# Conv plus GRU on one core: the start-up re-ordered (Toeplitz tile in quarters, biases by a product, weights in whole rows over two queues)

## The reference, cut to what matters

```python
x = x + conv(x, cond[:, None, :]) + conv_b          # causal, per channel
def cell(h, x):
    gi = x @ W_ih + b_ih                            # 512 -> 1536
    gh = h @ W_hh + b_hh
    r, z = sigmoid(i_r + h_r), sigmoid(i_z + h_z)
    n = tanh(i_n + r * h_n)
    return (1 - z) * n + z * h
x = x + scan(cell, cond, x)
```

## Time and profile before

| What | Value |
|---|---|
| median of 3 runs | 1174.54 us |
| the profiled execution: its time, its span | 1172.44 us, 1170.6 us |
| TensorE (matmul) busy | 1116.4 us, 95% of the span |
| VectorE / ScalarE / GpSimd busy | 797.3 / 535.8 / 441.1 us |
| moved by DMA | 101.65 MB |
| first matmul of the early product | 30.04 us after the span's start |

### The profile page before, as it was taken

One profiled execution on the slowest core, in us unless ns is written; L12 is line 12 of the kernel. 1 busy time (PEld: TensorE's weight loads), 2 busy tenths in 40 slices (PEclk: granted clock), 3 DMA queues, 4 the chain that ended last, 5 costly groups with the idle time before them and its releaser, 6 DMA issues.

```text
span 1170.6 us, 15057 instructions
## 1 busy us (share of the span) xinstructions
PE 1116.4 (95%) x5254; PEld 933.0 (80%) x5254; DVE 797.3 (68%) x1231; ACT 535.8 (46%) x1012; POOL 441.1 (38%) x734
## 2 busy tenths in 40 slices
PE   1999999999999599999999999999999999999996
PEld 1977888888888487888888888888888888888885
DVE  2746676676774646677777777777777777777774
ACT  3536776777774153243443333343344333344332
POOL 0352112122012724344455554444455554444332
PEclk9999999999999889999999999999999999999999
DMA  9999899888845401011111111111111111111101
GB/s 249 280 233 190 183 195 191 187 191 194 189 122 122 102 21 35 18 37 36 37 36 36 37 34 30 30 35 36 37 37 36 37 34 30 30 34 37 28 19 27
DMA packets 233228, 101.65 MB, mean 87 GB/s; under 512 B 212944, under 2 KB 217552, under 8 KB 231104
## 3 DMA queue, kind: packets, MB, share of 16 engines
q1 hardware_dynamic: 212544, 66.11, 25.8%
q0 software_dynamic: 16256, 33.32, 10.4%
q10 hardware_dynamic: 4352, 1.25, 0.4%
HBM read 66.49 MB, written 34.14 MB: 86 GB/s over the span
## 4 chain that ended last, share of the span: by engine, by line
PE 91%; DMA 3%; DVE 3%; ACT 1%; issue 1%; ACTq 1%; SPq 0%; POOL 0%; DVEq 0%; POOLq 0%
PE bank L1095 55%; PE bank L1142 26%; PE bank L1117 5%; PE bank L1057 2%; PE bank L1084 2%; DMA w_again<-in_L_cond_W_ih_dram 1%; DVE comb L902 1%; DMA early<-early_result 1%; ACT toep_early L665 0%; DMA xres<-stage 0%; DMA tap_pad<-tap_rows 0%; SPq L480 0%; ACTq L641 0%; DVE comb_lo L929 0%; DMA xT<-early 0%
## 5 line engine op out<-in xcount | busy, mean ns | idle before, releaser
L1095 PE MATMUL bank<-w_hh_hi,hT_hi 128*128 128x512 f32 x768 | 299.7, 390 | 0.1
L1095 PE MATMUL bank<-w_hh_lo,hT_hi 128*128 128x512 f32 x768 | 299.4, 390 | 0.0
L1095 PE MATMUL bank<-w_hh_hi,hT_lo 128*128 128x512 f32 x768 | 298.8, 389 | 0.0
L532 POOL DMA_DIRECT2D out_dram<-outZ x256 | 139.1, 550 | 248.5 <-DVE outZ L1040 246.3
L1095 PEld LDWEIGHTS bank<-w_hh_hi,hT_lo 128*128 128x128 f32 x768 | 144.2, 188 | 30.6
L1095 PEld LDWEIGHTS bank<-w_hh_hi,hT_hi 128*128 128x128 f32 x768 | 144.4, 188 | 28.5 <-issue 0.5
L1095 PEld LDWEIGHTS bank<-w_hh_lo,hT_hi 128*128 128x128 f32 x768 | 144.4, 188 | 27.6
L775 ACT ACTIVATE r<-bank 128x512 f32<-128x512 f32 x64 | 38.3, 598 | 205.6 <-PE bank L1095 204.8
L785 ACT ACTIVATE n_gate<-q 128x512 f32<-128x512 f32 x64 | 40.5, 634 | 197.9 <-DVE q L986 197.9
L525 POOL DMA_DIRECT2D xT<-xres x192 | 104.7, 550 | 19.6 <-issue 13.0
L1095 PE MATMUL bank<-w_ih_hi,xT_hi 128*128 128x512 f32 x240 | 97.1, 405 | 14.8 <-ACT bank L684 14.8
(11 more groups left out here) (140 smaller groups left out, 2193.8 us busy)
## 6 DMA issues: line engine op xcount, KB each, us to landing
x_unit<-in_x_dram SPq DMA_DIRECT2D x64, 256.0 KB, 5.1
toep_ring<-kernel_parts SPq DMA_DIRECT2D x128, 128.0 KB, 3.6
out_dram<-outZ POOLq DMA_DIRECT2D x256, 64.0 KB, 2.0
xres<-stage SPq DMA_DIRECT2D x32, 384.0 KB, 5.0
xT<-xres POOLq DMA_DIRECT2D x192, 64.0 KB, 2.1
early<-early_result SPq DMA_DIRECT2D x4, 1024.0 KB, 13.6
xT<-early POOLq DMA_DIRECT2D x60, 64.0 KB, 3.3
w_ih_raw<-in_L_cond_W_ih_dram SPq DMA_DIRECT2D x12, 256.0 KB, 7.5
```

The lines of the kernel that those rows point to most:

```text
L532: pool.dma_start(out[:, t, :].rearrange("(Q s) (q e) -> q s Q e", s=QUAD, e=P)[q4], outZ[t % 2][q4 * QUAD:(q4 + 1) * QUAD, :].rearrange("s ...
L1095: mm = nc.tensor.matmul(psum[:, :], a[:, rows], b[w][:, cols], start=False, stop=stop and n == 2, skip_group_check=True)
```

## The change

All of it lies in the start-up.

1. `toep_early` is built in four quarters by channel group: ScalarE makes three blocks of each, VectorE five. The early product waits, at each quarter of its groups, for that quarter only, and for `y0` only at the first group that writes the bank in which `y0`'s source lies. ScalarE makes `y0` after the first quarter.
2. The gate biases are loaded as two rows on two partitions and spread over the 128 partitions by four fp32 products with a small selecting tile (`bias_pick`); the products also open the gate banks. ScalarE copies the banks to the bias tiles (`keep_bias`). The four broadcasts, GpSimd's addition, the four opening matmuls and the four puts go.
3. `conv_b_rows`, `bias_d` and `bias_pair` are loaded on GpSimd's queue.
4. Each weight matrix is loaded in four DMAs of 32 partitions and whole rows (6 KB, 768 KB each) in place of twelve: partitions 0 to 63 on SyncE's queue, 64 to 127 on ScalarE's. ScalarE issues its two of `w_ih` after `y0`, before the second quarter of `toep_early`, and its two of `w_hh` after `kernel_parts`. `w_hh` on both queues waits for the four bias products. The rounding of a matrix waits for the whole of it.
5. VectorE evicts three banks before its first low part, then alternates nine low parts of `w_ih` with evictions, finishes the 16 evictions, and then does the nine low parts of `w_hh`.

```diff
-    bias_tmp = place("bias_tmp", N)
+    bias_pick = place("bias_pick", 3 * P, parts=2)
...
+    bias_rows = place("bias_rows", NG, parts=2)
...
-        def toep_early_block(c):
-
-            return toep_early[:, :].rearrange("p (g q u h) -> p q h u g", g=G0, q=QUADS, u=EARLY)[:, c // 2, c % 2]
+        ACT_BLOCKS = 3
+
+        def toep_early_block(c, n):
+            gs = slice(n * G0 // QUARTERS, (n + 1) * G0 // QUARTERS)
+            return toep_early[:, :].rearrange("p (g q u h) -> p q h u g", g=G0, q=QUADS, u=EARLY)[:, c // 2, c % 2, :, gs]
+
+        def tap_quarter(n):
+            gs = slice(n * G0 // QUARTERS, (n + 1) * G0 // QUARTERS)
+            return tap_blocks[:, :].rearrange("p (u g) -> p u g", g=G0)[:, :, gs]
...
+        def weights_quarter(w, q4):
+            return (raw[w][q4 * QUAD:(q4 + 1) * QUAD, :].rearrange("r (k n) -> r k n", k=KB),
+                    (w_ih, w_hh)[w][q4 * P:(q4 + 1) * P, :].rearrange("(k r) n -> r k n", r=QUAD))
...
-            def load_weights(w, matrix):
-                for g in GATES[w]:
-                    for q4 in range(QUADS):
-                        sp.dma_start(
-                            raw[w][q4 * QUAD:(q4 + 1) * QUAD, :].rearrange("r (k n) -> r k n", k=KB)[:, :, g:g + D],
-                            matrix[q4 * P:(q4 + 1) * P, g:g + D].rearrange("(k r) n -> r k n", r=QUAD),
-                        ).then_inc(raw_loaded[w][g // D], 16)
-
-            load_weights(0, w_ih)
-            for tile, source in ((bias_rz, b_ih[0:N]), (bias_tmp, b_hh[0:N]),
-                                 (bias_in, b_ih[N:NG]), (bias_hn, b_hh[N:NG])):
-                sp.dma_start(tile[:, :], source.partition_broadcast(P)).then_inc(bias_loaded, 16)
+            for q4 in range(QUADS // 2):
+                sp.dma_start(*weights_quarter(0, q4)).then_inc(raw_loaded[0], 16)
             sp.wait_ge(h0_by_k_ready, 1)
             sp.wait_ge(x_row_by_k_ready, 1)
-            load_weights(1, w_hh)
+            sp.wait_ge(bias_multiplied, 4)
+            for q4 in range(QUADS // 2):
+                sp.dma_start(*weights_quarter(1, q4)).then_inc(raw_loaded[1], 16)
             for n in range(QUARTERS):
                 sp.wait_ge(early_evicted, (n + 1) * NB0 // QUARTERS)
                 per = G0 // QUARTERS
@@ -497,11 +502,24 @@
...
+            nc.gpsimd.memset(bias_pick[:, 0:P], 1.0)
+            for row in range(2):
+                picked = nc.gpsimd.tensor_copy(bias_pick[:, (row + 1) * P:(row + 2) * P],
+                                               ident[0:2, row:row + 1].to_broadcast([2, P]))
+            picked.then_inc(bias_pick_set, 1)
             nc.gpsimd.memset(k_parts[:, :].bitcast(F32).rearrange("p (k j) -> p k j", j=P)[:, :, T:P],
                              0.0).then_inc(k_zeroed, 1)
 
-            pool.wait_ge(bias_loaded, 16 * 4)
-            nc.gpsimd.tensor_tensor(bias_rz[:, :], bias_rz[:, :], bias_tmp[:, :], ALU.add).then_inc(bias_rz_ready, 1)
+            pool.dma_start(conv_b_rows[:, :], conv_b.rearrange("(c g) -> c g", g=G0)).then_inc(conv_b_rows_loaded, 16)
+            for q4 in range(QUADS):
+                pool.dma_start(bias_d[q4 * QUAD:(q4 + 1) * QUAD, :],
+                               conv_b[q4 * P:(q4 + 1) * P].rearrange("(k r) -> r k", r=QUAD),
+                               allow_slow_non_contiguous=True).then_inc(bias_d_loaded, 16)
+            for c in range(2):
+                first = conv_b[c * UNIT:(c + 1) * UNIT]
+                pool.dma_start(bias_pair[c * T:(c + 1) * T, :].rearrange("s (n g) -> s n g", g=UNIT),
+                               bass.AP(first.tensor, first.offset, [[0, T], [2 * UNIT, NUNIT], [1, UNIT]])
...
+            for row, source in enumerate((b_ih, b_hh)):
+                act.dma_start(bias_rows[row:row + 1, :], source.rearrange("(o n) -> o n", o=1)).then_inc(bias_loaded, 16)
             act.wait_ge(tap_rows_ready, 1)
             act.dma_start(tap_pad[0:EARLY, :], tap_rows[:, :]).then_inc(tap_pad_stored, 16)
-            act.dma_start(conv_b_rows[:, :], conv_b.rearrange("(c g) -> c g", g=G0)).then_inc(conv_b_rows_loaded, 16)
             act.wait_ge(tap_pad_stored, 16 * 2)
             act.dma_start(tap_blocks[:, :].rearrange("p (u g) -> p u g", g=G0),
                           bass.AP(tap_pad.tensor, tap_pad.offset, [[G0, P], [D, EARLY], [1, G0]])
                           ).then_inc(tap_blocks_loaded, 16)
-            for q4 in range(QUADS):
-                act.dma_start(bias_d[q4 * QUAD:(q4 + 1) * QUAD, :],
-                              conv_b[q4 * P:(q4 + 1) * P].rearrange("(k r) -> r k", r=QUAD),
-                              allow_slow_non_contiguous=True).then_inc(conv_bias_loaded, 16)
-            for c in range(2):
-                first = conv_b[c * UNIT:(c + 1) * UNIT]
-                act.dma_start(bias_pair[c * T:(c + 1) * T, :].rearrange("s (n g) -> s n g", g=UNIT),
-                              bass.AP(first.tensor, first.offset, [[0, T], [2 * UNIT, NUNIT], [1, UNIT]])
-                              ).then_inc(conv_bias_loaded, 16)
...
             act.wait_ge(tap_blocks_loaded, 16)
             act.wait_ge(in_block_set, 1)
-            for c in range(C0 // 2):
-                nc.scalar.activation(toep_early_block(c), tap_blocks[:, :].rearrange("p (u g) -> p u g", g=G0),
-                                     ACT.Identity, scale=in_block[:, c:c + 1]).then_inc(toep_early_ready, 1)
-
-
-            act.wait_ge(conv_bias_loaded, 16 * (QUADS + 2))
-            act.wait_ge(x_row_done, 1)
-            for k in range(KB):
-                nc.scalar.activation(xT[0][:, k * P:(k + 1) * P], ps_x0[:, k * P:(k + 1) * P], ACT.Identity,
-                                     bias=bias_d[:, k:k + 1],
-                                     scale=k_full[:, k * P + T - 1:k * P + T]).then_inc(y0_ready, 1)
+            for n in range(QUARTERS):
+                for c in range(ACT_BLOCKS):
+                    nc.scalar.activation(toep_early_block(c, n), tap_quarter(n),
+                                         ACT.Identity, scale=in_block[:, c:c + 1]).then_inc(toep_early_ready, 1)
+                if n == 0:
+                    act.wait_ge(bias_d_loaded, 16 * QUADS)
+                    act.wait_ge(x_row_done, 1)
+                    for k in range(KB):
+                        nc.scalar.activation(xT[0][:, k * P:(k + 1) * P], ps_x0[:, k * P:(k + 1) * P], ACT.Identity,
+                                             bias=bias_d[:, k:k + 1],
+                                             scale=k_full[:, k * P + T - 1:k * P + T]).then_inc(y0_ready, 1)
+                    for q4 in range(QUADS // 2, QUADS):
+                        act.dma_start(*weights_quarter(0, q4)).then_inc(raw_act_loaded[0], 16)
...
 
             def high_weights(which):
+                act.wait_ge(raw_loaded[which], 16 * QUADS // 2)
+                act.wait_ge(raw_act_loaded[which], 16 * QUADS // 2)
                 for w, k, g in W_PARTS:
                     if w != which:
                         continue
-                    if k == 0:
-                        act.wait_ge(raw_loaded[w][g // D], 16 * QUADS)
                     cols = w_cols(k, g)
                     nc.scalar.activation(hi[w][:, cols], raw[w][:, cols], ACT.Copy).then_inc(w_hi_ready, 1)
 
+            act.wait_ge(h0_by_k_ready, 1)
+            act.wait_ge(x_row_by_k_ready, 1)
+            act.wait_ge(bias_multiplied, 4)
+            for q4 in range(QUADS // 2, QUADS):
+                act.dma_start(*weights_quarter(1, q4)).then_inc(raw_act_loaded[1], 16)
+
+            def keep_bias(bias, psum, done, n):
+                act.wait_ge(bias_multiplied, n)
+                nc.scalar.activation(bias, psum[:, :], ACT.Copy).then_inc(done, 1)
+
+            keep_bias(bias_rz[:, R:R + D], ps_r, bias_r_put, 1)
+            keep_bias(bias_rz[:, Z:Z + D], ps_z, bias_z_put, 2)
+            keep_bias(bias_in[:, :], ps_in, bias_in_put, 3)
+            keep_bias(bias_hn[:, :], ps_hn, bias_hn_put, 4)
             high_weights(0)
...
-            act.wait_ge(toep_early_dve_ready, C0 // 2)
+            act.wait_ge(toep_early_ready, ACT_BLOCKS * QUARTERS)
+            act.wait_ge(toep_early_dve_ready, (C0 - ACT_BLOCKS) * QUARTERS)
+            act.wait_ge(bias_pair_loaded, 16 * 2)
             high_weights(1)
...
             dve.wait_ge(tap_blocks_loaded, 16)
             dve.wait_ge(in_block_set, 1)
-            for c in range(C0 // 2, C0):
-                nc.vector.tensor_scalar(toep_early_block(c), tap_blocks[:, :].rearrange("p (u g) -> p u g", g=G0),
-                                        in_block[:, c:c + 1], None, ALU.mult).then_inc(toep_early_dve_ready, 1)
+            for n in range(QUARTERS):
+                for c in range(ACT_BLOCKS, C0):
+                    nc.vector.tensor_scalar(toep_early_block(c, n), tap_quarter(n),
+                                            in_block[:, c:c + 1], None, ALU.mult).then_inc(toep_early_dve_ready, 1)
```

(38 more changed lines are left out.)

18 lines of the change are left out of this document (7 added, 11 removed).

## The result

The changed kernel takes 1183.26 us (median of 4 runs, 1181.02 to 1186.0); the kernel before took 1172.95 beside it (4 runs). The ratio is 1.009, with a 95% interval of 1.0054 to 1.0127: 0.9% slower, where I forecast 0.37% faster and gave slower a chance of 0.04. The profiled execution took 1181.02 us (span 1179.2), 8.6 more than that of before.

What follows compares the result with a forecast made beforehand. It took the start-up to be bound by ScalarE's queue of copies, which set the early product's start at 30.04 us. Gains of 2.8 + 1.5 = 4.3 us took 1174.5 to 1170.2 us; range 1165.0 to 1174.5.

Steps and rivals of the forecast that it cites:

- Part 1: Start-up: bias loads off ScalarE's queue and toep_early in quarters; first quarter ready at 16.2 us, at most 7.8 us gained.
- the bound: Start of the early product: set by the landing of x_early, at 22.2 us, once the first quarter is ready earlier.
- Part 2: Weights on ScalarE's queue beside x_early: 1.57 MB delay its landing by 5 us, so the early product starts at 27.2.
- My count of packets one for one: DMA engines shared by both queues: packets alternate nearly one for one, as the 723 and 576 from 36 to 42 us.
- Part 3: Weight loading in partition halves: w_ih landed about 34.2 us, w_hh by about 41.5, no TensorE wait, cost 0.
- rival B: Weight halves serialize at 223 GB/s: w_ih complete about 41 us, bank 7 stalls 3.6, time 1174; chance 0.12.
- rival C: Early product: VectorE's low part ahead of eviction 4 stops TensorE; 1180 us or more; chance 0.03.
- Part 4: Bias products on TensorE: done by at most 20.6 us, ScalarE's bank copies by 29, cost 0.
- Part 5: Behind the early product's end: GpSimd's ring clearing starts at once, 1.5 us gained, bounds 0 and 2.7.
- Rival A: x_early is hardly delayed: start at 22.2 to 24.2 us, 7.3 to 9.3 us gained, 1165 to 1167; chance 0.33.

Runs made afterwards that it cites:

- e1: Changed kernel with ScalarE's halves of both weight matrices issued only after kernel_parts and the landing of x_early; ratio 0.9991.
- e2: Changed kernel with only ScalarE's w_hh half held until x_early has landed; ratio 1.0017.
- e10: Kernel before, with only the later reload of w_ih (w_again) as four whole-row DMAs, halves on SyncE's and ScalarE's queues; ratio 0.9957.
- e3: Changed kernel with all eight whole-row weight DMAs on SyncE's queue, behind x_early; 1175.32 us, ratio 1.0065.
- e5: e1 with VectorE's low parts of w_ih moved from behind evictions 3 to 11 to behind the last ones; 1171.89 us, ratio 1.0008 to the kernel before.
- e7: Changed kernel with weights loaded as before, 12 DMAs of 2 KB rows a matrix, all on SyncE's queue; ratio 0.9980.

## Why the prediction was wrong

**Part 1** was right up to the bound. In the changed kernel the first copy of `toep_early` starts at 14.9 us, and its first quarter is ready some 23.6 us before the product; with nothing in front of `x_early` the product starts at 22.04 (e1), where I had 22.2.

**Part 2 failed, and it alone turned the sign.** I charged 1.57 MB that come in at 20.4 us: 5 us. Measured: 18.1. Three things were off. ScalarE's `w_ih` issues stand at 15.05 us, not at 17.7, as its queue issues ahead of the copies of its own engine. Their first packets move at 17.0, not at 20.4, and the whole last DMA of `x_early`, 64 packets for each DMA engine, is held, where my working had about 20 left for each. `kernel_parts` (0.52 MB) on the same queue I used as evidence and never added. By itself it costs nothing (e1); behind `w_ih`, with `x_early` still in flight, all of it gets in. And I placed the issue of the `w_hh` half at about 26 us, where it was to come behind `x_early`, and counted none of it; it was issued at 21.05 and cost 9.0 us (changed kernel against e2). My count of packets one for one was right once both queues moved (844 to 850); what it was applied to was not. The delay feeds itself: each transfer that gets in early holds `x_early` in flight until the next is issued. The working took a landing to find out what collides with it, and did not go back when the landing moved.

**Part 3 failed in the rate.** Two halves add to 0.30 MB per us, not to 0.446, and in the changed kernel they never met. SyncE's half moved alone from 40 to 50:

```profile
40.00:50.00 10.00, 9.64 (x44) 9.35 (x45) 3.96 (x6) 2.04 (x4) 0.00 (x0) 1.00 1.02 205
```

`w_ih` was whole at 47.96 instead of 34.2. The late start hid this: with the product at 40.36, VectorE comes to its first low part when `w_ih` is there. With the start at 22 it is the next bound, 8.1 us in e1. So rival B was right about the lateness, rival C about the mechanism, and both only for a kernel whose start is early. For the changed kernel the slower side came by none of my rivals, but by Part 2's own term.

**Part 4** was right: the products ran from 13.8 to 20.9 us, their copies were done by 24.9, where I had 20.6 and 29, and TensorE waited for neither.

**Part 5** was right in its mechanism: the clearing stands at 68.82, 0.07 us behind the product's end, where before it was 1.45. That 1.7 us against 1.5 came out is in part luck. From the product's end to the convolution's last bank the kernel before takes 306.7 us and the changed one 305.5, but e10, whose start-up is that of the kernel before, takes 305.6: the 1.2 us lie within what two executions differ by. The other 0.5 come behind the last bank, where Part 5 has nothing.

**Rival A**'s place (start at 22 to 24) is reached by e1, e3, e5 and e7, and its price was wrong as well. I let each microsecond at the start reach the end. e5 ends the product 5.05 us early and keeps 0.7 at the convolution's last bank, e7 5.97 and keeps 2.8. Behind the product stand the store of `early`, the low parts of `w_hh` and the clearing. They wait for transfers, and for the rounding of a whole matrix, that do not come earlier with the product, and a wait of TensorE there costs clock as well (e7). Had `x_early` not been delayed, the change would have brought 0 to 4 us (by the profiled ends of e5, e1 and e7: 0.0, 1.4 and 3.7), not 7 to 9.

The sum with the measured terms: 7.8 us won by Part 1, less 18.1 of Part 2, plus the 1.7 behind the product is 8.6 us lost, as the profile has it. What stays open: why the last DMA of `x_early` does not begin while the first transfers of ScalarE's queue move, and why two halves give 0.30 and not 0.40. No run takes either apart.

## What to carry to other kernels

Put a large transfer on a second queue only after the landing that the path waits for, or count every byte issued on that queue before that landing, and count again with the later landing. Take a second queue for a reload that nothing urgent shares (e10), with the two queues on different halves of the partitions. And where VectorE has an operation of five times its usual length, look at what GpSimd does at that moment: one wait, put where GpSimd's work can start later, was worth nearly as much as the whole reload (5.7 us against 6.5 in the profiles).
